# Last feed-forward of a four-layer decoder: two-part f16 products, grouped attended rows, interleaved experts and weights asked for one stage earlier

## What is computed

```python
xn = (flat - mu) * rsqrt(var + 1e-05) * ln_scale + ln_bias
x_attn = xn @ attn_w.T + attn_b + flat            # 256 -> 256
xe = x_attn.reshape(2, 8, 128, 256)               # expert e takes rows e*128.. of each half
h = gelu(xe @ w1[e] + b1[e])                      # 256 -> 1024
eo = h @ w2[e] + b2[e]                            # 1024 -> 256
out = gelu(eo @ next_w.T + next_b)                # 256 -> 256
x = layernorm(x + out)                            # closing norm, the kernel's output
```

## Time and profile before

| | us |
|---|---|
| median of three executions | 3428.81 |
| the profiled execution | 3442.46 |
| its span, first to last instruction | 3440.7 |
| head of the last feed-forward, from its first moments to the first hidden product | 28.3 |
| from there to the end of the last expert's outputs | 152.7 |
| from there to the end of the span | 28.3 |

### The profile page before, as it was taken

One profiled execution on the slowest core, in us unless ns is written; L12 is line 12 of the kernel. 1 busy time (PEld: TensorE's weight loads), 2 busy tenths in 40 slices (PEclk: granted clock), 3 DMA queues, 4 the chain that ended last, 5 costly groups with the idle time before them and its releaser, 6 DMA issues. The chain is left out here.

```text
span 3440.7 us, 43169 instructions
## 1 busy us (share of the span) xinstructions
PE 2570.2 (75%) x14826; PEld 1451.9 (42%) x14826; DVE 1818.7 (53%) x5030; ACT 1327.1 (39%) x2732; POOL 982.2 (29%) x802
## 2 busy tenths in 40 slices
PE   6888885785725688888775688796776888669786
PEld 3323334563513233333452455473443333347575
DVE  4476655465748655555324568044332877546413
ACT  4335451453411266666413200224313455458521
POOL 1045660245256466666403200001001101103100
PEclk9979997897967799999987889897698799869898
DMA  3221101700545411111003000201002322030122
GB/s 106 71 58 40 40 2 34 250 23 14 165 124 94 107 29 44 43 37 36 14 18 75 11 16 12 107 4 29 13 0 76 39 27 27 12 94 2 57 99 74
DMA packets 185954, 182.60 MB, mean 53 GB/s; under 512 B 55449, under 2 KB 152474, under 8 KB 184974
## 3 DMA queue, kind: packets, MB, share of 16 engines
q1 hardware_dynamic: 176334, 167.35, 17.3%
q0 software_dynamic: 9408, 12.56, 2.4%
HBM read 121.68 MB, written 61.59 MB: 53 GB/s over the span
## 5 line engine op out<-in xcount | busy, mean ns | idle before, releaser
L929 POOL TENSOR_TENSOR l1a_p_lo<-res,l1a_p_hi 128x1024 f16<-128x1024 f32 x192 | 311.9, 1644 | 174.6 <-ACT res L1170 174.6
L1179 ACT ACTIVATE l0a_probs<-ps 128x1024 f32<-128x1024 f32 (+1 forms) x192 | 145.5, 810 | 175.4 <-PE ps L1033 103.1
L1179 ACT ACTIVATE l3a_probs<-ps 128x1024 f32<-128x1024 f32 (+1 forms) x192 | 146.9, 809 | 144.3 <-PE ps L1033 117.2
L1169 ACT ACTIVATE l1a_p_hi<-ps 128x1024 f16<-128x1024 f32 x192 | 157.8, 822 | 110.5 <-PE ps L1033 81.5
L1030 PE MATMUL ps<-l1a_qs,l1a_ks 128*128 128x512 f16 (+3 forms) x768 | 166.3, 331 | 32.1 <-ACT res L1170 32.1
L1201 DVE CUSTOM_DVE_ANT_0 l1a_masked<-ps,l1a_wide_mask 128x128 bf16<-128x128 f32 (+3 forms) x256 | 118.0, 490 | 102.9 <-PE ps L999 100.6
L999 PE MATMUL ps<-l1a_ks,l1a_qs 128*128 128x512 f16 (+3 forms) x384 | 121.3, 344 | 63.2 <-DVE l1a_nmax L1204 33.0
L954 POOL TENSOR_TENSOR l0a_both<-l0a_probs 128x768 f32<-128x768 f32 (+2 forms) x96 | 154.7, 1633 | 46.6 <-PE ps L1071 46.4
L2828 PE MATMUL ps<-x_m,x_x 128*128 128x462 f16 (+1 forms) x672 | 138.9, 355 | 31.3 <-PEq L111 30.7
L1170 ACT ACTIVATE res<-ps 128x1024 f32<-128x1024 f32 x192 | 158.1, 823 | 0.0
L1033 PE MATMUL ps<-mask_t,ident_b 128*128 128x128 bf16 x768 | 157.9, 225 | 0.0
(11 more groups left out here) (710 smaller groups left out, 6283.3 us busy)
## 6 DMA issues: line engine op xcount, KB each, us to landing
f_w<-in_L_ffn_w_dram SPq DMA_DIRECT2D x16, 1024.0 KB, 6.3
f_slots<-x0a_zeros SPq DMA_DIRECT2D x32, 256.0 KB
f_xe<-f_slots SPq DMA_DIRECT2D x32, 256.0 KB, 3.0
f_ys<-f_y SPq DMA_DIRECT2D x32, 256.0 KB
l1a_qs<-l_q_h SPq DMA_DIRECT2D x64, 128.0 KB
d_wall<-in_L_ffn_W_dram SPq DMA_DIRECT2D x3, 2112.0 KB
l0a_qs<-l_q_h SPq DMA_DIRECT2D x32, 128.0 KB
l0a_ks<-l_k_h SPq DMA_DIRECT2D x16, 256.0 KB
```

The costliest lines, as they stand in the source:

```text
L929: pool.tensor_tensor(ph_lo[:, n % SLOTS, :, 0:w], probs[:, n % FULL, :, 0:w], ph_hi[:, n % SLOTS, :, 0:w], ALU.subtract).then_inc(s_["low_ ...
L1169: act.activation(ph_hi[:, n % SLOTS, :, 0:w], SB[n % 2][:, :, 0:w], ACT.Exp)
L1179: act.activation(probs[0:KR, n % SLOTS, 2 * pr:2 * pr + 2, 0:w], SB[x % 2][:, :, 0:w], ACT.Exp).then_inc(s_["exps"], 1)
```

## The change

The last two stages become one call, in which the objects that the feed-forward needs are made ahead of `x3a`:

- `LastExperts` holds the f32 weights of two experts and all constants. `cross_rows` calls `following.begin(sp)` behind the loads of `x3a_v`, so that the constants and two experts' weights are asked for while `x3a` runs. Biases of all experts come in one load each.
- Every f32 operand is split in two f16 parts, upper and lower, and each product becomes three f16 products (`TERMS`: upper by upper, and the two mixed ones). The upper part is a copy to f16, the lower one a subtraction. Weights: ScalarE and GpSimd, in 4 chunks of 1024 an expert. Hidden values: both on VectorE. Attended rows, groups of 512: ScalarE and VectorE; normalised rows: ScalarE and GpSimd.
- Attended rows are computed once by groups of 512 rows, two groups ahead of the experts and two between them (order of groups 0, 2, 1, 3, since experts 0 to 3 need only groups 0 and 2).
- Experts are interleaved on TensorE: hidden products of expert e, following product of e - 1, outputs of e.
- The closing norm is done expert by expert on VectorE between the experts. The scaling of experts 0 to 4 is GpSimd's, that of 5 to 7 is shared with VectorE. Rows are stored by expert. The stage `f3o` and its barrier are gone.

```diff
-def cross_rows(k, name, H, shared, ms, vp, xs, bo=None, keep=None):
+def cross_rows(k, name, H, shared, ms, vp, xs, bo=None, keep=None, following=None):
...
+                if following:
+                    following.begin(sp)
...
+class LastExperts:
+    def load(self, sp, e):
+        a, half = self.k.a, DC * self.HID
+        sp.dma_start(self.wf[:, e % 2, 0:half].rearrange("p (c n) -> p c n", c=DC), a["L3_ffn_w1"][e].rearrange("(c p) n -> p c n", p=P)).then_inc(self.s[f"ld{e % 2}"], 16)
+        sp.dma_start(self.wf[:, e % 2, half:2 * half].rearrange("p (c n) -> p c n", n=D), a["L3_ffn_w2"][e].rearrange("(c p) n -> p c n", p=P)).then_inc(self.s[f"ld{e % 2}"], 16)
+    def begin(self, sp):
+        self.constants(sp)
+        for e in range(2):
+            self.load(sp, e)
...
+    ORDER = (0, 2, 1, 3)
+    EARLY = 5
+    TERMS = [(0, 0), (0, 1), (1, 0)]
...
+            def _(sp):
+                for e in range(2, E):
+                    sp.wait_ge(s_["w_lo"], 4 * (e - 2) + 4)
+                    given.load(sp, e)
...
+            def _(pool):
+                def lower_weights(e, i):
+                    pool.wait_ge(s_["w_hi"], 4 * e + i + 1)
+                    pool.tensor_tensor(chunk(wp[1], e, i), chunk(given.wf, e, i), chunk(wp[0], e, i), ALU.subtract).then_inc(s_["w_lo"], 1)
...
+                for e in range(E - 1):
+                    for i in range(4):
+                        lower_weights(e + 1, i)
+                    if e in (0, 2):
+                        lower_rows(2 + e // 2)
+                pool.wait_ge(s_["rs_ready"], 1)
+                for e in range(EARLY):
+                    scaled(e, 0)
+                    scaled(e, 1).then_inc(s_["pool_out"], 1)
...
+            def _(pe):
...
+                turn(0)
+                turn(1)
+                attend(0)
+                attend(1)
+                for e in range(E):
+                    hidden(e)
+                    if e:
+                        following(e - 1)
+                    if e in (0, 2):
+                        turn(2 + e // 2)
+                    if e in (1, 3):
+                        attend(2 + e // 2)
+                    outputs(e)
+                following(E - 1)
...
+            def _(act):
...
+                for e in range(E):
+                    for p in range(4):
+                        hidden(e, p)
+                        if p % 2 and e + 1 < E:
+                            upper_weights(e + 1, p // 2)
+                    if e:
+                        outputs(e - 1)
+                    if e in (0, 2):
+                        columns(2 + e // 2)
+                    if e in (1, 3):
+                        upper_rows(2 + e // 2)
+                    for i in (2, 3) if e + 1 < E else ():
+                        upper_weights(e + 1, i)
+                    if e == EARLY + 1:
+                        roots(1, 0, EARLY)
...
+            def _(dve):
...
+                def hidden(e, p):
+                    x = 4 * e + p
+                    dve.wait_ge(s_["hid_ready"], x + 1)
+                    dve.tensor_copy(hp[0][:, p, :], hid[:, p, :]).then_inc(s_["hid_hi"], 1)
+                    dve.wait_ge(s_["hid_hi"], x + 1)
+                    dve.tensor_tensor(hp[1][:, p, :], hid[:, p, :], hp[0][:, p, :], ALU.subtract).then_inc(s_["hid_lo"], 1)
...
+                normed(2)
+                normed(3)
+                attended(0)
+                lower_rows(0)
+                attended(1)
+                lower_rows(1)
+                for e in range(E):
+                    for p in range(4):
+                        hidden(e, p)
+                    if e:
+                        following(e - 1)
+                    if e in (1, 3):
+                        attended(2 + e // 2)
+                    if e:
+                        residual(e - 1)
+                    if e in (1, 3):
+                        lower_rows(2 + e // 2)
+                    if e == EARLY:
+                        variances(0, EARLY)
+                    if e == EARLY + 2:
+                        inverses(1, 0, EARLY)
+                    outputs(e)
```

More of the change, by code:

```diff
@@ L3048, in _, with fused_cross @@
                     router.number(dve, NG - 1)
-def fused_cross(k, name, H, DH, wqt, wk, wv, wo, scale, bo=None, norm=None, shared=False, own=None, route=None):
+def fused_cross(k, name, H, DH, wqt, wk, wv, wo, scale, bo=None, norm=None, shared=False, own=None, route=None, ahead=None):
     sets = 1 if shared else B
@@ L3063, in fused_cross @@
             cross_operators(k, f"{name}c", H, DH, shared, ms, vp, wqt, wk, wv, wo, scale, norm, (xnt, *own) if own else None, xs)
-        cross_rows(k, f"{name}a", H, shared, ms, vp, xs, bo, route)
+        following = ahead() if ahead else None
+        cross_rows(k, f"{name}a", H, shared, ms, vp, xs, bo, route, following)
+    return following
 def l0_cross_attention(k, route):
@@ L3085, in l2_cross_attention, with l3_cross_attention @@
                 64 ** -0.5, bo=a["L2_xattn_bo"])
-def l3_cross_attention(k, x_in, x_out):
+def l3_cross_attention(k, keep):
     a = k.a
-    fused_cross(k, "x3", 16, 64, a["L3_xattn_Wq"], a["L3_xattn_Wk"], a["L3_xattn_Wv"], a["L3_xattn_Wo"],
-                64 ** -0.5, norm=a["L3_xattn_norm_c"], own=(a["L3_xattn_g_x"], a["L3_xattn_b_x"]))
+    return fused_cross(k, "x3", 16, 64, a["L3_xattn_Wq"], a["L3_xattn_Wk"], a["L3_xattn_Wv"], a["L3_xattn_Wo"],
+                       64 ** -0.5, norm=a["L3_xattn_norm_c"], own=(a["L3_xattn_g_x"], a["L3_xattn_b_x"]), ahead=lambda: LastExperts(k, keep))
 def top_mask(dve, ph, ch, sel, m8, K, E, tmp, mask):
@@ L3898, in _, with __init__, tile, constants @@
                 normal(NG - 1)
-def l3_feed_forward(k, x_in, x_out):
-    nc, a = k.nc, k.a
+class LastExperts:
     E, HID = 8, 1024
+    def __init__(self, k, keep):
+        self.k, E, HC = k, self.E, self.HID // P
+        def tile(name, shape):
+            return keep.enter_context(k.nc.sbuf_tensor(f"f3_{name}", shape, F32, side="right"))
+        self.wf = tile("wf", [P, 2, 2 * DC * self.HID])
+        self.cf = tile("cf", [P, 2, DC, D])
+        self.bat, self.bnx = tile("bat", [P, DC]), tile("bnx", [P, D])
+        self.b1, self.b2 = tile("b1", [P, E, HC]), tile("b2", [P, E, DC])
+        self.wb = tile("wb", [P, 2, DC])
+        self.s = {n: k.nc.alloc_semaphore(f"f3_{n}") for n in ("c_ld", "ld0", "ld1")}
+        self.sems = list(self.s.values())
+        self.n_c = 16 * 8
+    def constants(self, sp):
+        a = self.k.a
+        for dst, src in ((self.cf[:, 0], weight_rows(a["L3_ffn_attn_w"])), (self.cf[:, 1], weight_rows(a["L3_ffn_next_w"])), (self.bat[:], a["L3_ffn_attn_b"]),
+                         (self.bnx[:], a["L3_ffn_next_b"]), (self.b1[:], a["L3_ffn_b1"].rearrange("e p c -> p e c")), (self.b2[:], a["L3_ffn_b2"].rearrange("e p c -> p e c")),
+                         (self.wb[:, 0, :], a["L3_ffn_ln_scale"]), (self.wb[:, 1, :], a["L3_ffn_ln_bias"])):
+            sp.dma_start(dst, src).then_inc(self.s["c_ld"], 16)
+    def load(self, sp, e):
[6 more added lines that the diff above has]
+            self.load(sp, e)
@@ L3906, in l3_feed_forward @@
+def l3_feed_forward(k, given, x_out):
+    nc = k.nc
+    E, HID = given.E, given.HID
     HC = HID // P
     TW = 2 * P
[L3908 to L4017 removed]
@@ L4021, with l3_cross_and_feed_forward @@
+def l3_cross_and_feed_forward(k, x_in, x_out):
+    with ExitStack() as keep:
+        given = l3_cross_attention(k, keep)
+        l3_feed_forward(k, given, x_out)
 class Kernel:
@@ L4064 @@
 STAGES = [l0_self_attention, l0_cross_to_l1_self_attention, l1_cross_attention, l1_feed_forward,
-          l2_self_attention, l2_cross_attention, l2_feed_forward, l3_self_attention, l3_cross_attention, l3_feed_forward]
+          l2_self_attention, l2_cross_attention, l2_feed_forward, l3_self_attention, l3_cross_and_feed_forward]
 def build(nc, a, out, stages):
```

275 lines of the change are left out of this document (239 added, 36 removed).

## The result

The changed kernel takes 3407.11 us in the median of six executions (3395.65 to 3412.85), the kernel before 3438.73 in six (3423.49 to 3442.55). The ratio is 0.9908 with an interval of 0.9889 to 0.9927: faster by 0.9%, 31.6 us. The forecast was 47.3 us less.

The account below looks back on a forecast made before the run. TensorE's f32 rate was taken to bound the experts, VectorE the tail. Head 26.5, middle 120 and tail 15.5 make 162 us against 209.3, 47.3 less, from the median 3428.81: 3381.5 us (3370 to 3395, full range 3355 to 3412).

Parts of the forecast that it names:

- the clock falls in every round: Rival, experts: TensorE's clock falls each round, rounds of 17.5 to 20 us, middle 135 to 150, 3396.5 to 3411.5; chance 0.18.
- slower: Rival, experts: TensorE stays at 1.2 GHz through the whole loop, middle 199.7 us, stage 243, total 3462.5; chance 0.05.
- Products: TensorE, experts: three f16 products take 0.33 us against 0.44 for one f32; 11.8 us per expert, 100.6 for the middle.
- The blocking: Experts: VectorE's instructions on SBUF stand still during GpSimd's subtractions; a round in the middle takes 15.0 us (12.8 to 18.5).
- Experts: Middle, first hidden product to last outputs: 120 us (103 to 150) where 152.7 stood.
- Head: Stretch ahead of the first hidden product: 26.5 us (25 to 31) where 28.3 stood, set by VectorE's order.
- norms of groups 0 and 2 are ready at 7.1: Head: these norms done 7.1 us in, VectorE's first sum of attended rows at 18.5, first hidden product at 26.5.
- Tail: Stretch behind the last outputs: 15.5 us (13.5 to 19) where 28.3 stood, with GpSimd scaling three times 0.7.
- Early loads: Weights and constants asked for in the stage ahead: cost nothing, up to 1 us; the head's 7.25 us wait goes.
- weights early is no gain: Rival, head: it has its own chain and comes out at 31 us, 4.5 more; total 3386.

Follow-up runs that it names:

- experiment 1: Changed kernel with GpSimd's subtractions of the experts' weights cut to 16 of every 1024 columns, lower parts cleared by a MEMSET: experts 101.8 us, 3377.04 us in one execution.
- experiment 2: Changed kernel with the Gelu written back to PSUM, where VectorE copies and subtracts from: experts 103.6 us, stage 154.2, 3382.07 us in one execution.
- Experiment 7: Changed kernel with VectorE's norms of groups 2 and 3 moved into the first expert's loop: head 27.6 us, first round 21.8, stage 175.9; 3402.31 us in one execution.
- experiment 4: Changed kernel's structure with hidden, outputs and following products back in f32, unsplit: stage 168.1 us, median 3398.35 us, ratio 0.9877 to the kernel before.
- experiment 8: Changed kernel with GpSimd's 13 last scalings cut to 5, VectorE taking the rest: tail 12.7 us, stage 170.7, 3400.8 us in one execution.
- experiment 10: Experiment 2, Experiment 7 and experiment 8 combined, plus a new head order with norms behind the first two experts' hidden values: stage 148.3 us, 3380.56 us, ratio 0.982 to the kernel before.

## Why the prediction was right, and where it was off

Direction, the full range (3355 to 3412) and the mechanism among the experts held; the value, 3381.5, was 25.6 us low against 3407.11. That lies outside the narrower range of 3370 to 3395, which had a chance of 0.52, and inside the 3396.5 to 3411.5 of the rival *the clock falls in every round*. This rival still isn't what happened: it needs a middle of 135 to 150 us, and the middle took 125.4, with three falls of the clock in eight rounds. Of the 25.6 us, 9.9 are the median it was subtracted from: 3428.81 in three executions, 3438.73 in six. The sum has 13.6 us too few for the stage, in all three terms. The last 2.1 are the difference between the 33.7 us of the stage and the 31.6 of the medians. Two slips of the prediction changed nothing: the rival *slower* adds up to 241.7 us, not 243, and the full range starts from a middle of 100 us, under the 100.6 that TensorE alone was to take.

- **Products** held. Without gaps a late round takes 11.8 us (experiments 1 and 2), as worked out, and the experts 101.8 to 103.6 against 100.6 and 103. Twelve attended products in a row among the experts took 2.75 us, 0.23 each, above even the 0.21 taken from the row of before; the 131 ns of the Trainium skill ("TensorE: Matmul & The Clock Gate", Back-to-back issue gap) are not borne out.

```profile
3271.94 2.75 PE L4071 MATMUL ps<-f_x,f_c 128*128 128x512 f16 x12
```

- **The blocking** held, in kind and in size: a round in the middle, forecast at 15.0 us within 12.8 to 18.5, came at 16.3, 12.2 and 17.7 (mean 15.4), alternating as forecast. The open question, whether copies are held as well, is answered by the 2.36 us copies. The Trainium skill ("SBUF — State Buffer", Who interferes with whom) has them held, and the trace agrees. One reading of the earlier trace rows was not exact: of the two GpSimd instructions there only the first subtracts, the second adds; both have two SBUF inputs.
- **Experts, 5.4 us short** (120 against 125.4). Two terms. The first round was taken at 12.6 us and at full clock; it took 14.7, because its first 5.7 us ran at 0.50: the clock fell in the 3.19 us that TensorE waited for its last input. (In those 5.7 us 27 products were recorded, 0.21 us each instead of 0.11.) Rounds 1 to 3 came at 15.6, 18.1 and 18.8, 52.5 us instead of 49.7; there the clock fell once (round 2), and once more in each of two later rounds (4 and 6).

```profile
3250.60:3256.30 5.70, 5.65 (x27) 4.04 (x28) 1.12 (x2) 1.19 (x4) 0.00 (x0) 0.50 0.00 0
```

- **Head, 5.8 us short** (26.5 against 32.3), outside its bounds, 25 to 31. The step that failed is "norms of groups 0 and 2 are ready at 7.1", and what was built on it: they were ready at 10.0. The blocking was applied to the experts and left out of the head. There VectorE's TENSOR_SCALARs with one tensor input in SBUF were held too, even one of 128x4 values. The Trainium skill ("SBUF — State Buffer", Who interferes with whom) names tensor_scalar beside the copy; the trace agrees.

```profile
3220.17 1.41 DVE L4216 TENSOR_SCALAR f_n_ve<-f_n_mv 128x4 f32<-128x4 f32 x1
...
3223.77 3.06 DVE L4225 TENSOR_SCALAR f_r<-res,f_n_mv,f_n_rs 128x256 f32<-128x256 f32 x4
...
3232.01 1.64 DVE L4216 TENSOR_SCALAR f_n_ve<-f_n_mv 128x4 f32<-128x4 f32 x1
...
3236.09 4.96 DVE L4225 TENSOR_SCALAR f_r<-res,f_n_mv,f_n_rs 128x256 f32<-128x256 f32 x4
```

  Undisturbed these take 0.17 and, four together, 1.38 us. The excess is 1.2 + 1.7 + 1.5 + 3.6 = 8.0 us; VectorE's first sum of attended rows stood at 24.2 us, not 18.5, and the 8.1 from there to the first hidden product are as forecast. Experiment 7 shows that the norms of the last two groups stand in the head's way (27.6 with them moved). What the holding costs is read from the durations above and not shown by itself: experiment 4, with GpSimd nearly out of the head, has 22.9, but the splits of weights and attended rows are gone there too.
- **Tail, 2.3 us short** (15.5 against 17.8), inside its bounds. GpSimd's scaling was taken at 0.7 us; it takes 1.22, and thirteen in a row set the end:

```profile
3374.83 15.86 POOL L4027 TENSOR_SCALAR res<-f_r,f_mv,f_rs 128x256 f32<-128x256 f32 x13 [8.84 <-DVE f_rs L4273]
```

  They end at 3390.7, 3.2 us ahead of the last store's landing. Ten of them, of experts 0 to 4, start 1.2 us ahead of the end of the last outputs and end at about 3387.0 (10 x 1.22), while the last roots are inverted at 3382.7. At 0.7 us they would have been done in time and only three would have stood on the path, as the prediction had it. With VectorE's help the tail is 12.7 (experiment 8).
- **Early loads** at 0 to 1 us: the cross-attention was 0.6 us longer, within its scatter. The rival *weights early is no gain* came near the head in size (31 against 32.3) but not in cause: without them it is 45.1.

The prediction's account lacked a comparison with f32 in the new structure. Experiment 4 shows that the term it gave most room, the f16 products, is given back almost whole by the standstill and the longer head that its splitting makes.

## What to carry to other kernels

A split into f16 parts moves time from TensorE to the elementwise engines. Before building it, look at which of VectorE's instructions will stand beside a GpSimd instruction on SBUF. Here its copies, its TENSOR_SCALARs with an SBUF source and its subtractions with two were held by GpSimd's subtractions, once per instruction, down to one of 128x4 values; its moments, reciprocals and everything with a source in PSUM were not. A source in PSUM avoids it for 0.25 us a copy. Moving a held instruction elsewhere in time (experiments 7 and 10) gave nothing, since it met GpSimd again. Measure the new structure with the old arithmetic as well: here it was worth the whole gain.

## What the runs showed of the hardware

- Not every VectorE instruction that reads SBUF is held. In the head of the kernel after, four moment instructions beside GpSimd's subtractions took 1.39 us together, as alone, while the TENSOR_SCALAR of 128x4 just ahead of them took 1.41 instead of 0.17:

```profile
3219.43 2.12 POOL L4030 TENSOR_TENSOR f_c<-f_cf,f_c 128x1024 f16<-128x1024 f32 x1 [14.18 <-ACT f_c L4173]
...
3220.17 1.41 DVE L4216 TENSOR_SCALAR f_n_ve<-f_n_mv 128x4 f32<-128x4 f32 x1
3221.49 1.39 DVE L4211 BATCH_NORM_STATS2 f_n_stats<-res 128x6 f32<-128x256 f32 x4
3221.51 4.20 POOL L4018 TENSOR_TENSOR f_w<-f_wf,f_w 128x1024 f16<-128x1024 f32 x2
```

- A GpSimd MEMSET, which only writes SBUF, holds as well. In experiment 1 one of 6.93 us stood at the head. Moments ran beside it unhindered (three in 1.06 us), then a TENSOR_SCALAR that takes 0.17 us alone stood until the MEMSET ended, and four moments behind it stood with it:

```profile
3225.40 6.93 POOL L4029 MEMSET f_w<- 128x8192 f16 x1 [11.73 <-POOLq L111]
...
3225.78 1.06 DVE L4213 BATCH_NORM_STATS2 f_n_stats<-res 128x6 f32<-128x256 f32 x3
...
3227.29 5.06 DVE L4218 TENSOR_SCALAR f_n_ve<-f_n_mv 128x4 f32<-128x4 f32 x1
3227.37 4.98 DVE L4213 BATCH_NORM_STATS2 f_n_stats<-res 128x6 f32<-128x256 f32 x4
```

- GpSimd's TENSOR_SCALAR holds far less than its subtraction. Beside the thirteen scalings of the tail, of 1.22 us each, a VectorE TENSOR_TENSOR with two SBUF inputs took 0.69 us, as alone (0.81 and 0.84 in experiments 2 and 4), and VectorE's own scalings 0.51 us in the mean, up to 0.64, where the same form takes 0.41 alone. In experiment 8, five of them beside GpSimd took 2.29 us together, and six behind its end 2.03. The Trainium skill ("SBUF — State Buffer", Who interferes with whom) has two SBUF inputs contend with a GpSimd instruction that reads SBUF, under an exclusive lock; the traces do not bear that out for this one, since none of these instructions stood for a whole scaling. Why a scaling differs from a subtraction stays open. (The last row below gives busy us and mean ns of one.)

```profile
3380.31 0.69 DVE L4259 TENSOR_TENSOR f_r<-f_pre,res 128x512 f32<-128x512 f32 x1 [0.69 <-ACT f_pre L4166]
...
L4309 DVE TENSOR_SCALAR res<-f_r,f_mv,f_rs 128x256 f32<-128x256 f32 x3 | 1.4, 508 | 0.0
```
